# The high half of gelu's output is copied by ScalarE instead of VectorE, in the first stage of a macaron layer

## The reference

```
x = x + 0.5 * ffn(layernorm(x))
x = x + attn(layernorm(x))        # in-projection, conv, silu, dt, scan over 2048 steps, out-projection
x = x + 0.5 * ffn(layernorm(x))

def ffn(x):                        # w1: 1024 x 256, w2: 256 x 1024
    h = gelu(x @ bin(w1).T + b1)   # bin(w) = mean|w| per row * sign(w)
    return h @ bin(w2).T + b2
```

## Time and the profile before

| | |
|---|---|
| median of 3 runs | 1534.88 us (1534.82 to 1535.24) |
| profiled execution, its time | 1534.2 us |
| profiled execution, its span in the trace | 1532.4 us |
| first stage, scan and last stage | to about 428 us, to about 1300 us, to the end |
| TensorE (PE) busy | 1446.3 us, 94% of the span |
| VectorE (DVE) busy | 1253.5 us, 82% |
| ScalarE (ACT) busy | 1119.2 us, 73% |
| GpSimd (POOL) busy | 941.0 us, 61% |

### The profile page before, as it was taken

The page is one execution under the profiler, slowest core; times in us unless marked ns, Lnnn a source line. Parts: engine busy times, 40 slices in busy tenths (PEclk is TensorE's granted clock), DMA queues, the critical chain, the costliest instruction groups (busy, mean ns, idle before and its releaser), DMA issues.

```text
span 1532.4 us, 25717 instructions
## 1 busy us (share of the span) xinstructions
PE 1446.3 (94%) x7022; PEld 1019.1 (67%) x7022; DVE 1253.5 (82%) x2526; ACT 1119.2 (73%) x2618; POOL 941.0 (61%) x956
## 2 busy tenths in 40 slices
PE   6999999999879999999999999999999998999998
PEld 5555555555467777777777777777666666677776
DVE  7776566745479999999999999999999999788884
ACT  4454455445999999999999999999999964334243
POOL 0224323432269999999999999999999998400000
PEclk9999999999999999999999999999999999999999
DMA  8224427444747666666657666566544347465520
GB/s 269 83 70 155 145 95 198 134 163 128 240 133 208 170 165 189 168 171 167 171 158 187 181 162 180 157 175 169 137 110 110 98 102 234 121 218 186 157 77 28
DMA packets 232326, 236.30 MB, mean 154 GB/s; under 512 B 46296, under 2 KB 198040, under 8 KB 232184
## 3 DMA queue, kind: packets, MB, share of 16 engines
q1 hardware_dynamic: 231240, 233.34, 52.9%
q10 hardware_dynamic: 944, 1.31, 0.2%
HBM read 136.31 MB, written 98.56 MB: 153 GB/s over the span
## 4 chain that ended last, share of the span: by engine, by line
DVE 35%; POOL 14%; PE 12%; issue 5%; DVEq 1%; POOLq 1%; DMA 1%; ACT 0%; SPq 0%; ACTq 0%
DVE h L1344 22%; POOL rc L1108 13%; DVE banks L1334 9%; PE banks L1493 4%; PE banks L1514 3%; PE banks L1524 3%; DVE qs L1328 2%; PE banks L1168 1%; DVEq L1342 1%; DMA ub<-scratch_ub 1%; DVE q_ln_st L1770 1%; DVE q_g L1679 1%; POOLq L1116 1%; DVE q_x L1651 1%; PE banks L1534 0%
## 5 line engine op out<-in xcount | busy, mean ns | idle before, releaser
L1344 DVE TENSOR_TENSOR_SCAN h<-decay,banks 128x352 f32<-128x352 f32 x820 | 710.4, 881 | 57.2 <-DVE banks L1334 2.9
L1119 POOL TENSOR_TENSOR hc<-h,bc 128x640 f32<-128x640 f32 x410 | 592.5, 1445 | 0.0
L1168 PE MATMUL banks<-hc,w_ident 128*128 128x320 f32 (+1 forms) x1664 | 525.7, 439 | 0.1
L1237 ACT ACTIVATE tb<-dtc,a 128x320 f32<-128x320 f32 (+1 forms) x832 | 417.5, 556 | 4.8 <-DVE x L611 4.8
L1168 PEld LDWEIGHTS banks<-hc,w_ident 128*128 128x128 f32 x1664 | 284.5, 191 | 70.2 <-issue 0.4
L1259 ACT ACTIVATE decay<-tb 128x640 f32<-128x640 f32 x410 | 295.2, 724 | 0.0
L1108 POOL TENSOR_TENSOR rc<-qs,w_mhalf 128x1 f32<-128x1 f32 x410 | 224.9, 549 | 107.0 <-DVE qs L1328 107.0
L1154 PE MATMUL banks<-ub 128*128 128x176 f32 x1640 | 272.2, 288 | 2.1 <-DMA ub<-scratch_ub 2.0
L1147 PEld LDWEIGHTS banks<-sc_ss,sc_ones 128*128 128x128 f32 x820 | 123.3, 189 | 158.1 <-ACT sc_sq L1248 151.3
L1154 PEld LDWEIGHTS banks<-ub 128*128 128x128 f32 x1640 | 216.4, 192 | 2.4 <-DMA ub<-scratch_ub 2.3
L1147 PE MATMUL banks<-sc_ss,sc_ones 128*128 128x1 f32 x820 | 151.6, 254 | 37.7 <-ACT sc_sq L1248 19.0
(11 more groups left out here) (133 smaller groups left out, 1812.5 us busy)
## 6 DMA issues: line engine op xcount, KB each, us to landing
ub<-scratch_ub SPq DMA_DIRECT2D x410, 107.5 KB
bc<-scratch_blk SPq DMA_DIRECT2D x205, 160.0 KB, 3.5
scratch_ub<-turned SPq DMA_DIRECT2D x64, 512.0 KB, 3.5
scratch_ub<-spread SPq DMA_DIRECT2D x64, 176.0 KB, 2.4
scratch_xc<-xc SPq DMA_DIRECT2D x8, 1024.0 KB, 4.8
scratch_sg<-sg SPq DMA_DIRECT2D x8, 1024.0 KB, 5.8
piece<-scratch_u SPq DMA_DIRECT2D x32, 256.0 KB, 4.0
q_ys<-scratch_y SPq DMA_DIRECT2D x8, 1024.0 KB, 5.6
```

The costliest lines, as they stand in the source:

```text
L1119: pool.tensor_tensor(hc[:, pl % 2, :, at * S:(at + 1) * S] .rearrange("p (c b n) e -> p c b n e", c=KE, b=B)[:, :, b], state(m)[:, :, 0:S] ...
L1168: mm = pe.matmul(banks[:, y_bank(p), 0:KE * B * wide], w.ident[:], rhs, start=(n == 0), stop=(n == N - 1))
L1237: act.activation(tanh_rows(c, r), dtc[:, c % 2, k * B:(k + 1) * B, 0:blocks_of(c) * S].rearrange("p b (k e) -> p k b e", e=S), ACT.Tanh, s ...
L1344: dve.tensor_tensor_scan(state(m).rearrange("p r e -> p (r e)")[:, half], decay[:, m % DRING, half], psI[m % B][:, half], 0.0, ALU.mult, A ...
```

## The change

VectorE no longer casts. ScalarE makes the high half with a Copy activation, one gelu later: gelu m, then the copy of m - 1, and the last copy at the end of the group. The copy of a tile's first block waits until the previous tile's `down` has read `g`, which VectorE waited for before.

```
+        def high_g(i, m):
+            act.wait_ge(ring_read, use["up", i, m] + 1)
+            if i >= 1 and m == 0:
+                act.wait_ge(dn_done, KD * i)
+            act.activation(g[:, 0, m, :], gf[:, m % GF, :], ACT.Copy).then_inc(split_hi, 1)
+
         def gelus(i, m0, m1):
             for m in range(m0, m1):
                 src = held(("up", i, m))
...
                 act.activation(gf[:, m % GF, :], src, ACT.Gelu, bias=w.b1[:, m:m + 1],
                                scale=w.a1[:, m:m + 1]).then_inc(ring_read, 1)
+                if m > m0:
+                    high_g(i, m - 1)
+            high_g(i, m1 - 1)
...
         def split_g(i, m0, m1):
-            if i >= 1 and m0 == 0:
-                dve.wait_ge(dn_done, KD * i)
             for m in range(m0, m1):
-                dve.wait_ge(ring_read, use["up", i, m] + 1)
-                dve.tensor_copy(g[:, 0, m, :], gf[:, m % GF, :]).then_inc(split_hi, 1)
                 dve.wait_ge(split_hi, KH * i + m + 1)
                 dve.tensor_tensor(g[:, 1, m, :], gf[:, m % GF, :], g[:, 0, m, :].bitcast(F32),
                                   ALU.subtract).then_inc(split_lo, 1)
```

## The result

| | before | after |
|---|---|---|
| median of 4 runs each, side by side | 1535.06 us (1534.82 to 1536.23) | 1527.29 us (1525.78 to 1529.85) |
| the same kernels again, 29 and 12 runs | 1533.92 us (1530.77 to 1537.78) | 1530.75 us (1525.67 to 1533.07) |
| profiled execution, time and span | 1534.2, 1532.4 us | 1527.76, 1526.0 us |

The first comparison gives a ratio of 0.995 (95% interval 0.9932 to 0.9967), 7.8 us; the second, made later with many more runs, 0.9973 (0.9962 to 0.9984), 3.2 us. The change is faster; how much is in good part a matter of which runs are looked at, and most of this study is about that.

What follows compares the result with a forecast made beforehand. TensorE was taken to set the first stage's pace, so time could be won only in its waits or clock. -2.76 + 1.43 - 1.70 = -3.03 us took 1534.9 to 1531.9 us, range 1529.6 to 1534.6.

Steps and rivals of the forecast that it cites:

- the clock term: TensorE's gate projections: of three taking 8.83 us, one would return to 7.13 behind shorter waits, -1.70 us.
- I carry the difference through one to one: Stages behind the first start when it ends, so its gain was passed on unchanged to the total.
- the loss ahead of the loop: Tiles 0 and 1: ScalarE's copies delay the first x projection by 1.43 us, 0.69 of it from tile 0.
- The chain: Steps 1 to 6, VectorE, ScalarE, TensorE: without the cast, gelu 4 and gate projection come 0.46 us earlier each, -2.76 us.
- the copies' price: ScalarE: one copy takes 0.62 us, filling 0.51 us of the queue; gelu and copy together 1.18 us.
- the start of the x projection: Tile 0's x projection, waiting for the copy `zT` at 46.19, starts at 47.51 in place of 46.08.
- the whole 1.43 us: Step 0: the x projection's delay stays in full, +1.43 us, as nothing else makes TensorE wait there.
- Rival D: ScalarE becomes the pace if a copy takes 0.93 us or more: 1538 us and up, chance 0.04.
- the bounds that I took from the earlier trace, 1.55 and 2.37: Idle us before gate projections: none up to 1.55 preceded 8.83 us; 2.37 was the shortest that did.
- the seven casts of a tile that are not in the chain: VectorE's casts behind block 0: removing them brings nothing, as TensorE sets the pace behind gelu 4.
- the forecast's -3.03: Whole kernel: the sum -2.76 + 1.43 - 1.70 = -3.03 us.

Runs made afterwards that it cites:

- first_only: Kernel before, with ScalarE copying only block 0 of tiles 2 to 7, the other 58 casts staying on VectorE; 1526.80 us, ratio 0.9953.
- extra_cast: Kernel before, with a second VectorE cast of block 0 ahead of the first subtraction in tiles 2 to 7; 1537.72 us, ratio 1.0023.
- loop_only: Kernel before, with ScalarE copying all blocks of tiles 2 to 7 and VectorE still casting tiles 0 and 1; 1529.56 us, ratio 0.9969.
- after_again: The changed kernel itself, unaltered, run again later beside others on the same chip; 1530.75 us.
- one_more: One unread VectorE memset added ahead of the loop: to the kernel before, 1532.31 us; to the changed kernel, 1533.16 us, repeated at 1528.88.
- late_warm_before: Kernel before, casts still on VectorE, plus unread matmuls in TensorE's idle time and one VectorE memset more; 1523.52 us, ratio 0.9936.

## Why the prediction was right, and where it failed

The profiled execution came out 6.4 us shorter (-2.6 + 1.4 - 3.4 - 1.8), the forecast had 3.0. Two steps make the difference: the clock term "I take one: -1.70" was -3.40, and "I carry the difference through one to one" left out 1.3 us within the scan and 0.5 behind it. A third, on what stays of the loss ahead of the loop, was wrong too, and the clock hid it. The chain and the copies' price were right.

**The chain: right.** "What is taken out of it ahead of gelu 4 is taken out of TensorE's wait": six waits, 13.4 to 10.8 us, each shorter by 0.39 to 0.46. first_only shows that one copy of a tile carries it all, extra_cast that the chain also lengthens.

**The copy and the start of the x projection: right. What stays of the loss: wrong.** 630 ns for the 620 taken, two in a row in 1.15 to 1.17 (0.51 of queue forecast, 0.53 measured), gelu and copy 1.18 us apart. The copy `zT` started at 46.13 (46.19 forecast) and the x projection at 47.47 (47.51). But "In step 0 nothing else makes TensorE wait, so the whole 1.43 us" stay fails beside loop_only: TensorE waits there 0.30 us for `xn` behind the x projection, and 0.86 us of the loss stay. Rival D, ScalarE as the pace, never came near its bound of 0.93 us for a copy. The `xT` of step 2 stood 5.27 us behind gelu 4 (5.3 forecast), and nothing waited for it. TensorE's wait on `sg` ahead of the last dt projection is 4.4 us as before; ahead of the others there is none.

**The clock: right in kind, mis-sized.** "I take one: -1.70." The profiled execution had two stretches less, 3.40 us. One step was missing in my reasoning: I counted only gate projections, while the x projection of tile 0 also stood at 8.83 before, in a row that I quoted for another purpose. More deeply, the count of such stretches is not fixed by the kernel; only how often they come is. The same changed kernel had the x projection at 7.13 and two gate projections at 8.83 in one profile, and in after_again's these:

```profile
46.80 8.83 PE L354 MATMUL banks<-zT,win 128*128 128x512 f32 x16 [1.72 <-ACT zT L453]
...
153.12 7.13 PE L354 MATMUL banks<-zT,win 128*128 128x512 f32 x16 [2.24 <-ACT gf L437]
...
202.08 7.13 PE L354 MATMUL banks<-zT,win 128*128 128x512 f32 x16 [2.20 <-ACT gf L437]
...
298.95 8.83 PE L354 MATMUL banks<-zT,win 128*128 128x512 f32 x16 [2.24 <-ACT gf L437]
```

Idle time of 1.98 us was followed by a stretch at 1.2 GHz in one execution, and idle time of 2.24 was and was not. So the bounds that I took from the earlier trace rows, 1.55 and 2.37, do not sort single projections. They do mark where the share changes (15 of 16 from 2.37 us on, 9 of 23 at 1.98 to 2.24, none of 42 up to 1.89): shortening the waits does win clock, on average 1.4 us by the runs' mean clock. So -1.70 was a fair value for the mean and, as a term of one execution, a draw. In the four kernels with filled idle time the waits ahead of these projections were at most 1.3 us (1.75 in late_warm_before), and every one took 7.13. The Trainium skill (TensorE: Matmul & The Clock Gate, section What's actually happening) says that the phase differs from run to run; these runs agree, at 1525.7 to 1533.1 us for one program. My range left that scatter out, which 3 runs of the kernel before (1534.8 to 1535.2) did not show and 81 (1530.8 to 1544.4) did.

**"I carry the difference through one to one": failed.** Within the scan another 1.3 us came, and 0.5 behind it. The scan's part (1.1 of it by the 781st scan instruction, where the clock is still the same) goes with VectorE's pauses, which the change removed because it took 64 casts and one semaphore wait off VectorE ahead of the scan, from an even number to an odd one. Both one_more kernels show in their traces that the number alone does this, for 1.8 to 2.2 us; that the pair itself gained less is not explained, but the even and the odd kernels differ among themselves by 1 us and more. I priced the seven casts of a tile that are not in the chain at nothing; in the first stage that holds, but as a count they mattered behind it.

**Against the two medians.** By the sum of terms that stand, -2.6 + 0.9 - 1.7 (pauses, the mean over the traces) = -3.4, near the 3.9 at equal clock, and the clock comes on top with what a run happens to have: 1.4 us on average, twice that and more in the profiled execution. The later 12 runs are 3.2 us below by their median and 4.3 by their mean. That the forecast's -3.03 agrees with the later 3.2 us is luck: it holds one clock stretch where the pauses belonged, and the median of 12 scattered runs shows 1.1 us less than their mean. The 7.8 us of the first four runs, clocks 0.992 to 0.994, were runs with few such stretches; of the 16 runs of the changed kernel five had 0.991, at 1531.2 us.

**Open.** That even or odd decides follows from where the pauses fall. What happens on VectorE at the numbers that are 64 more than a multiple of 128 is not shown, nor whether other instructions at these numbers lose time. The 0.5 us behind the scan are within what that stage differs by between kernels that do not touch it (213.2 to 214.1 us), and were not traced further. The levels at equal clock give the loop's part as 4.0 us (3.6 on its own chip) where the traces give 2.6; that difference of about the method's error is not explained.

## What to carry to other kernels

In a hand-ordered pipeline look for the one instruction of each round that stands between two engines' hand-over; moving six of 64 casts gave what moving all gave, and spared the cost ahead of the loop. When TensorE is 94% busy and a projection sometimes takes 8.83 us in place of 7.13, first fill the idle time ahead of it with matmuls that nobody reads, and only then judge small changes, on a profile whose clock is steady. Compare kernels both by their mean over many runs and by runs of the same granted clock: the second takes the scatter out, and with it what the change itself wins or loses through the clock. Look in stages that an edit does not touch: an instruction more or less ahead of them can move a pause there.

## What was unexpected of the hardware

- VectorE pauses by 0.35 us (0.82 between two starts in place of 0.47) every 384 of its instructions in the scan, six or seven times, when 570, 586, 618, 628, 634 or 640 of its instructions stand ahead of it, and not up to 1260 us with 569, 629 or 635. Each of the 53 pauses in fourteen traces stands at an instruction whose number is 64 more than a multiple of 128, and none of 5684 scan instructions of the same kind at another number has one.
- A stretch at 1.2 GHz cost 1.70 us of a projection of 7.13 and followed idle times from 1.0 to 3.0 us, and below 2.7 us not always: 15 of 16 gate projections behind 2.37 to 3.01 us, 9 of 23 behind 1.98 to 2.24, none of 42 behind less.
- Six unread matmuls a step, and eight ahead of the loop, took 6.8 us off the kernel before.
